# Four kinds of transposes moved from TensorE to VectorE blocks and HBM, in a four-layer graph network

## The chip, the cores and the metric

The kernel runs on one core of one Trainium2 chip. The metric is the device time of one execution in microseconds (us), median of several runs. The engines of the core are named PE (TensorE; PEld is its weight load), DVE (VectorE), ACT (ScalarE), POOL (GpSimd) and SP (SyncE, which here only issues DMAs). All data are float32.

## The reference, cut to what matters

Four layers, each followed by a residual and a normalization over the 128 features; 32 batches of 256 nodes.

```python
x = _layernorm(x + _L0_gnn_ref(x, adj, ...))      # gated neighbours and biases
x = _layernorm(x + _L1_gnn_ref(x, adj, ...))      # two linear maps, two norms over all rows
x = _layernorm(x + _L2_gnn_ref(x, adj, W, a))     # attention
x = _layernorm(x + _L3_gnn_ref(x, adj, ...))      # two graph maps, then LSTMs over windows of 1 to 4
# _L2_gnn_ref
Wh = h @ W;  s1 = Wh @ a1;  s2 = Wh @ a2
e = s1[:, :, None] + s2[:, None, :]
e = where(e >= 0, e, 0.2 * e);  e = where(adj == 0, -inf, e)
out = softmax(e, axis=-1) @ Wh
# _L3_gnn_ref
h = relu(adj @ (x @ Wg0 + bg0));  h = relu(adj @ (h @ Wg1 + bg1))
for p in 1..4:
    last = lstm_p(h cut in windows of p nodes)     # p steps, each needs the one before
    h[every p-th node] = last
```

## The kernel before

The 32 batches are 8 groups of 4 (`GB`). One group is 128 partitions x 1024 elements: 8 tiles of 128x128, two halves of nodes for each of 4 batches. Layers 0 and 1 run first for all groups (they need norms over all rows), to about 144 us. Then the attention of groups 0 and 1 runs alone (the front, to about 188 us). Then come the turns: `slots(slot)` calls `slot(s, ...)` for s = 2 to 10, and in turn s four groups are in work at once: the attention of group s (functions `a_...(s)`), the two graph maps of layer 3 of group s-1 (`a_spread0`, `a_weigh0`, `a_weigh1`, `a_spread1`), the LSTM of group s-2 (11 steps k = 0 to 10; `lstm_x` is the input part and `lstm_h` the state part of the gates, written x(k) and h(k) below) and the last norm of group s-3 (`t_...`). Turns 2 to 7 have an attention, turns 8 and 9 have only what is left; turn 9 splits each LSTM step into two lanes.

An LSTM step goes PE (gates, PSUM `QQ`), ACT (L1200, tanh of the gates), DVE (L1680 to L1690, cell), ACT (L1236, tanh of the cell), DVE (L1708, state), and then PE again. Every engine runs its instructions in the order in which its function `slot` is written, and waits on semaphores. The order of a turn is written out by hand, the same for turns 3 to 7.

In a turn PE also makes four kinds of transposes, each a 128x128 block against the identity `ident`, into PSUM, from where DVE reads them:
- `a_residual` (L680), 8 blocks: the output of layer 1, which lies as features x nodes in `O2T`. DVE adds the residual (L1552, into `Z`), takes statistics (L1400) and dot products with two vectors (L1570); ACT applies the norm (L1042, into `X2`).
- `a_rows` (L729), 8 blocks: the attention's s2, one column per tile, turned into rows of 1024 that stand on all partitions. `a_max` (L1587) reads them.
- `a_turn_e` (L746), 16 blocks: the unnormalized attention weights `E1`. DVE copies them to `MS` (L1608, `a_weights`), and `a_mix` (L767) multiplies with them; `a_project_mix` (L777) follows, `a_sum2_mix` on DVE adds the residual, then come statistics, a power -0.5 on POOL (L446, `rstd`) and the application on POOL (L512, `scale2`), which the next turn's `a_spread0` (L786) reads.
- `t_turn` (L884), 8 blocks: the LSTM's result in `HT`. DVE adds the residual (L1779, `t_sum`), and POOL applies the last norm (L525, `tail`).

SP stores each finished group to the output. Nothing else is moved by DMA in the turns.

## Time and profile before

| what | us |
|---|---|
| median of 3 runs (637.57 to 638.1) | 638.07 |
| the profiled execution | 637.48 |
| its span, first to last instruction | 635.7 |
| PE busy in that span | 621.7 (98%) |
| DVE, ACT, POOL busy | 469.7, 433.1, 168.9 |
| granted TensorE clock | 0.996 of full speed |

The turns start at 188.4 us; turns 2 to 7 take 57.2 to 57.7 us each, turn 8 takes 50.7 and turn 9 with the end about 52. Busy time of PE is modelled and says that it has work, not that it computes at its peak. In the listings of a timeline a row that has xN stands for N instructions, and the distance from its start to the start of the next row is what they cost when PE never waits.

### The profile page before, as it was taken

The numbers are of one execution on the slowest core, as the hardware profiler recorded it, in microseconds if no ns is written. First come the engines' busy times: TensorE is split into PE (matmuls) and PEld (weight loads), VectorE is DVE, ScalarE is ACT, GpSimd is POOL, SyncE is SP. The second block draws the span as 40 slices with busy tenths as digits, with TensorE's granted clock in tenths as the row PEclk, the third lists the DMA queues.
The fourth block names the chain that finished last, engine by engine and source line by source line (L and its number), as shares of the span: only waits on it lengthen the run. The fifth ranks groups of instructions, "written<-read, shape, count | busy, mean of one in ns | idle before, by whom it ended". The sixth has DMA issues, their size and how long they took to land.

```text
span 635.7 us, 9580 instructions
## 1 busy us (share of the span) xinstructions
PE 621.7 (98%) x2768; PEld 441.7 (69%) x2768; DVE 469.7 (74%) x1623; ACT 433.1 (68%) x995; POOL 168.9 (27%) x228
## 2 busy tenths in 40 slices
PE   9999999999999999999999999999999999999994
PEld 6756656447975687579658766865885687577794
DVE  4999999877857657866886687588668766465656
ACT  3667767866947766785677577657847766546774
POOL 1464551005233002303603240341143032103201
PEclk9999999999999999999999999999999999999998
DMA  8334000000000000000000000000000000000000
GB/s 342 129 123 167 1 1 1 1 0 2 2 1 1 0 2 1 1 2 33 2 0 2 33 2 2 34 2 1 1 33 2 2 32 2 1 1 34 2 35 34
DMA packets 4372, 16.84 MB, mean 26 GB/s; under 512 B 480, under 2 KB 480, under 8 KB 4192
## 3 DMA queue, kind: packets, MB, share of 16 engines
q1 hardware_dynamic: 4320, 16.23, 6.6%
q8 instruction: 22, 0.36, 0.2%
q14 instruction: 30, 0.25, 0.1%
HBM read 12.03 MB, written 4.19 MB: 26 GB/s over the span
## 4 chain that ended last, share of the span: by engine, by line
PE 77%; DVE 3%; ACT 2%; issue 1%; POOL 0%; POOLq 0%; ACTq 0%; DVEq 0%
PE QQ L831 27%; PE QQ L843 15%; PE PA L814 4%; PE PA L786 4%; PE PB L805 2%; PE PB L796 2%; PE PB L667 2%; PE PA L667 2%; PE PB L767 2%; PE PA L767 2%; PE QQ L865 1%; PE PB L884 1%; PE PA L746 1%; PE PB L746 1%; PE QQ L875 1%; PE PA L777 1%
## 5 line engine op out<-in xcount | busy, mean ns | idle before, releaser
L1200 ACT ACTIVATE raw<-QQ,BL 128x256 f32<-128x256 f32 (+2 forms) x279 | 150.3, 559 | 78.5 <-PE QQ L843 39.9
L831 PE MATMUL QQ<-HT,WT 128*128 128x256 f32 (+2 forms) x558 | 183.5, 473 | 0.8 <-DVE HT L1708 0.4
L446 POOL TENSOR_TENSOR RSD<-VAR,pw 128x4 f32<-128x4 f32 (+1 forms) x43 | 62.0, 1443 | 379.1 <-DVE VAR L1422 379.1
L831 PEld LDWEIGHTS QQ<-HT,WT 128*128 128x128 f32 x558 | 103.9, 190 | 58.2 <-issue 29.7
L843 PE MATMUL QQ<-HB,WT 128*128 128x256 f32 (+2 forms) x336 | 100.1, 441 | 0.2
L843 PEld LDWEIGHTS QQ<-HB,WT 128*128 128x128 f32 x336 | 61.2, 190 | 28.8 <-issue 13.4
L1236 ACT ACTIVATE raw<-raw 128x256 f32<-128x256 f32 (+4 forms) x79 | 37.0, 469 | 22.8 <-DVE raw L1690 18.8
L1680 DVE SCALAR_TENSOR_TENSOR raw<-raw 128x256 f32<-128x256 f32 (+2 forms) x60 | 31.9, 532 | 22.7 <-ACT raw L1200 21.9
L1708 DVE SCALAR_TENSOR_TENSOR HB<-raw 128x256 f32<-128x256 f32 (+4 forms) x42 | 19.9, 474 | 25.1 <-ACT raw L1236 25.1
L512 POOL TENSOR_SCALAR X<-four,MEAN,RSD 128x128 f32<-128x128 f32 x64 | 32.8, 526 | 1.6
L1042 ACT ACTIVATE X<-Z,OFF,RSD 128x128 f32<-128x128 f32 x80 | 31.8, 482 | 2.0 <-POOL OFF L452 2.0
L622 PE MATMUL PA<-AHT,X 128*128 128x256 f32 x128 | 29.5, 384 | 1.6 <-ACT X L1042 1.5
L1163 ACT ACTIVATE HB<-HB,EB 128x256 f32<-128x256 f32 x64 | 30.9, 502 | 0.2
L622 PEld LDWEIGHTS PA<-AHT,X 128*128 128x128 f32 x128 | 23.7, 190 | 9.6 <-issue 6.4
L786 PE MATMUL PA<-AD,X 128*128 128x256 f32 x128 | 30.3, 379 | 0.0
L636 PE MATMUL QQ<-one_b,later 128*128 128x512 f32 x64 | 29.1, 598 | 0.2 <-ACT one_b L1071 0.2
L814 PE MATMUL PA<-AD,Y 128*128 128x256 f32 x128 | 29.2, 380 | 0.0
L525 POOL TENSOR_SCALAR four<-HB,MEAN,RSD 128x128 f32<-128x128 f32 x56 | 28.8, 530 | 0.7
L786 PEld LDWEIGHTS PA<-AD,X 128*128 128x128 f32 x128 | 23.8, 191 | 6.8 <-issue 4.1
L814 PEld LDWEIGHTS PA<-AD,Y 128*128 128x128 f32 x128 | 24.2, 190 | 4.3
L1083 ACT ACTIVATE HB<-QQ 128x512 f32<-128x512 f32 x32 | 17.9, 587 | 12.7 <-PE QQ L636 12.5
L599 PE MATMUL PB<-four,AD 128*128 128x512 f32 x56 | 26.1, 609 | 0.0
(249 smaller groups left out, 1173.9 us busy)
## 6 DMA issues: line engine op xcount, KB each, us to landing
four<-in_x SPq DMA_DIRECT2D x8, 512.0 KB, 3.9
raw<-in_xt SPq DMA_DIRECT2D x8, 512.0 KB, 6.3
out<-four SPq DMA_DIRECT2D x7, 512.0 KB, 2.6
WT<-in_lstm SPq DMA_DIRECT2D x1, 2048.0 KB, 9.3
later<-in_later SPq DMA_DIRECT2D x1, 725.5 KB, 10.1
AD<-in_adj SPq DMA_DIRECT2D x2, 256.0 KB, 4.6
out<-four SPq DMA_DIRECT2D x2, 256.0 KB, 2.0
early<-in_early SPq DMA_DIRECT2D x1, 275.0 KB, 4.5
```

What stands on the lines that cost most here:

```text
L446: pool.tensor_tensor(RSD[kk][:, ts], VAR[kk][:, ts], pw[:, ts], ALU.pow).then_inc(ln[k]["rstd"], some)
L512: pool.tensor_scalar(tile_of(X1, g, c, b), nth(f.Z2, t), MEAN[f.kk2][:, t:t + 1], RSD[f.kk2][:, t:t + 1], ALU.add, ALU.mult).then_inc(ln[2 ...
L622: mm = pe.matmul(PA[:, b * NODES:(b + 1) * NODES], tile_of(X1, g, m, b), AHT[:, m, :], start=(m == 0), stop=(m == NC - 1))
L786: mm = pe.matmul(PA[:, b * NODES:(b + 1) * NODES], tile_of(X1, g, m, b), ADJT[:, m, :], start=(m == 0), stop=(m == NC - 1))
L814: mm = pe.matmul(PA[:, b * NODES:(b + 1) * NODES], turned(Y, m, b), ADJT[:, m, :], start=(m == 0), stop=(m == NC - 1))
L831: mm = pe.matmul(steps_view(Q[q], k), WT[:, 0, (p - 1) * 4 + q, :], ht_view(par, k), start=True, stop=(s == 0))
L843: pe.matmul(Q[q][:, 0:nw * GB], WT[:, 1, (p - 1) * 4 + q, :], HS[:, (k - 1) % 2, 0:nw * GB], start=False, stop=True).then_inc(g_ps, 1)
L1042: act.activation(nth(to, t), nth(z, t), ACT.Identity, bias=OFF[kk][:, t:t + 1], scale=RSD[kk][:, t:t + 1]).then_inc(ln[k]["out"], 1)
L1163: e = act.activation(f.E1[:, t], f.E1[:, t], ACT.Exp, bias=f.EB[:, t:t + 1], scale=1.0, accum_out=DEN[:, t:t + 1] if g > 1 else None)
L1200: act.activation(TG[q][:, at:n], Q[q][:, at:n], ACT.Tanh, scale=0.5 if q == G else 0.25, bias=BL[:, p - 1, q:q + 1]).then_inc(g_ok, 1)
L1236: act.activation(TC[:, at:n], CELL[:, at:n], ACT.Tanh, scale=0.5).then_inc(tc_ok, 1)
L1680: dve.scalar_tensor_tensor(out=target[:, 0:n], in0=TG[I][:, 0:n], scalar=1.0, in1=TG[G][:, 0:n], op0=ALU.add, op1=ALU.mult).then_inc(cell_ ...
```

## The change

Four kinds of 128x128 transposes leave PE in turns 2 to 7 (the first three) and 3 to 9 (the LSTM's). Each becomes: a DVE instruction that transposes all 32x32 blocks of a buffer (`STREAM_TRANSPOSE`), a DMA that stores the buffer to a scratch in HBM, a wait of SP for it, and four DMAs of 32 partitions each that load it back with the blocks in their new places. The s2 row goes so too, but small (8 rows of 32 elements out, then one row of 1024 broadcast to 128 partitions into `ROWS`).

```diff
+            def y_through(g):
+                sp.wait_ge(y_blk, g - 1)
+                sp.dma_start(turn_y[g], YD).then_inc(y_put, 16)
+                sp.wait_ge(y_put, 16 * (g - 1))
+                reach(sp, z1_ok, NC * (g - 2))
+                for q in range(P // QUAD):
+                    sp.dma_start(quad_rows(YF, q), quad_source(turn_y[g], q)).then_inc(y_got, 16)
...
+            def r_through(g):
+                sp.wait_ge(r_blk, g - 1)
+                for q in range(P // QUAD):
+                    sp.dma_start(turn_r[g].rearrange("(t q i) -> q t i", t=TILES, i=QUAD)[q],
+                                 S2T[q * QUAD:q * QUAD + TILES, :]).then_inc(r_put, 16)
+                sp.wait_ge(r_put, 64 * (g - 1))
...
+                sp.dma_start(ROWS, turn_r[g:g + 1, :].broadcast_to([P, COLS])).then_inc(r_got, 16)
+            def slot(s, par, A, B, L, T):
+                g = s - 3
+                if T and g < LAST:
+                    t_through(g)
+                if s + 2 < GROUPS:
+                    y_through(s + 2)
+                if A:
+                    e_through(s, 0)
+                    e_through(s, 1)
+                    r_through(s + 1) if s + 1 < GROUPS else None
...
-            def a_residual(g, h=None):
-            def a_rows(g):
-            def t_turn(g, par):
...
                 for b in some:
-                    pe.wait_ge(pt_ok, GB * (g - 1) + b + 1)
+                    pe.wait_ge(e_got, 64 * (2 * (g - 2) + b // 2 + 1))
...
+            def a_s12(g):
...
+                dve.transpose(S2T[:], S12[:, TILES:]).then_inc(r_blk, 1)
...
+            def e_blocks(g, some):
+            def t_blocks(g):
+            def y_blocks(g):
```

The two sums that DVE made from PSUM (L1552, L1779) go to POOL (`y_sum`, `t_sum`, two instructions of 128x512 each), and so does the application of the first norm, eight instructions of ACT (L1042) in a turn (`scale1`). The first norm and the dot products of group s+1 are made in turn s, those of group 2 in the front. The LSTM's factor 0.5 is folded into `a_spread` and the small norm steps. All engines get a new order in a turn; `a_mix` of batch 3 and the projections of batches 2 and 3 move to the turn behind.

Below, the order of PE over the border of two full turns, first before (from the mixes of batches 0 to 2 to the first spread of the next turn). L831 is x(k), L843 is h(k).

```order
L767 MATMUL PB<-HB,X 128x256 x2
L767 MATMUL PA<-HB,X 128x256 x2
L767 MATMUL PB<-HB,X 128x256 x2
L777 MATMUL PB<-later,one_a 128x128 x2
L777 MATMUL PA<-later,one_a 128x128 x2
L843 MATMUL QQ<-HB,WT 128x256 x4
L831 MATMUL QQ<-HT,WT 128x256 x4
L767 MATMUL PA<-HB,X 128x256 x2
L777 MATMUL PB<-later,one_a 128x128 x2
L843 MATMUL QQ<-HB,WT 128x256 x4
L777 MATMUL PA<-later,one_a 128x128 x2
L831 MATMUL QQ<-HT,WT 128x512 x3
```

The same stretch and on to the second spread of the next turn in the changed kernel; there L951 is x(k), L963 is h(k), L889 the mix, L899 its projection, L907 the spread and L917 `a_weigh0`.

```order
L963 MATMUL QQ<-HB,WT 128x256 x4
L951 MATMUL QQ<-HT,WT 128x512 x3
L889 MATMUL PA<-HB,X 128x256 x2
L951 MATMUL QQ<-HT,WT 128x512 x3
L899 MATMUL PB<-later,one_a 128x128 x2
L907 MATMUL PA<-AD,X 128x256 x4
L899 MATMUL PA<-later,one_a 128x128 x2
L951 MATMUL QQ<-HT,WT 128x512 x7
L963 MATMUL QQ<-HB,WT 128x512 x4
L917 MATMUL PB<-one_b,later 128x512
L907 MATMUL PA<-AD,X 128x256 x4
L951 MATMUL QQ<-HT,WT 128x340 x7
```

The transposes at L680, L884 and L729 that stood in this stretch are gone, the last mix and two projections stand in it now, and the second spread stands behind h(3). Next, DVE over the same border in the changed kernel: the small scores (L1984) with their block transpose (L1988), the cell of step 10, the small norm steps of `scale2`'s first half, the state of step 10, the cell of step 0 and the first `a_max` of the new turn (ISA, L2000).

```order
L1984 TENSOR_TENSOR S<-DOT,RSD 128x16
L1988 STREAM_TRANSPOSE S2T<-S 128x32
L2099 SCALAR_TENSOR_TENSOR raw<-raw 128x256
L2105 SCALAR_TENSOR_TENSOR raw<-raw 128x256
L2109 SCALAR_TENSOR_TENSOR raw<-raw 128x256
L1823 TENSOR_TENSOR SUM<-STL 128x8
L1824 TENSOR_TENSOR DIF<-STL 128x4
L1826 TENSOR_TENSOR SQD<-DIF 128x4
L1827 TENSOR_SCALAR MEAN<-SUM 128x4
L1829 SCALAR_TENSOR_TENSOR SQD<-SQD,SUM 128x4
L1833 TENSOR_SCALAR VAR<-SQD 128x4
L2127 SCALAR_TENSOR_TENSOR HT<-raw 128x64x4
L2099 SCALAR_TENSOR_TENSOR raw<-raw 128x512
L2000 ISA HB,MX<-WH,NEG 128x256
```

Before, the small scores and `a_max` stood in one turn, with `a_rows` of PE between them. Last, POOL from the first norm's power for group s+1 to that sum in the next turn. Before:

```order
L446 TENSOR_TENSOR RSD<-VAR,pw 128x8
L525 TENSOR_SCALAR four<-HB,MEAN,RSD 128x128 x8
L446 TENSOR_TENSOR RSD<-VAR,pw 128x4
L512 TENSOR_SCALAR X<-four,MEAN,RSD 128x128 x4
L446 TENSOR_TENSOR RSD<-VAR,pw 128x4
L512 TENSOR_SCALAR X<-four,MEAN,RSD 128x128 x4
```

In the changed kernel (L534 the power, L600 `scale2`, L613 the last norm, L592 the scaling of layer 1's output, L632 `scale1`, L640 `t_sum`, L621 `y_sum`):

```order
L534 TENSOR_TENSOR RSD<-VAR,pw 128x4
L600 TENSOR_SCALAR X<-four,MEAN,RSD 128x128 x4
L534 TENSOR_TENSOR RSD<-VAR,pw 128x8
L613 TENSOR_SCALAR four<-HB,MEAN,RSD 128x128 x8
L592 TENSOR_SCALAR HB<-HB,BN 128x1024
L632 TENSOR_SCALAR X<-Z,MEAN,RSD 128x128 x8
L534 TENSOR_TENSOR RSD<-VAR,pw 128x4
L600 TENSOR_SCALAR X<-four,MEAN,RSD 128x128 x4
L640 TENSOR_TENSOR HB<-HB,X 128x512 x2
L621 TENSOR_TENSOR HB<-HB,X 128x4x128 x2
```

Between the two halves of `scale2` there now stand the last norm, the scaling and the first norm's application.

## Rows read from the trace of the kernel before

**Rows 1.** The page's part 1: busy time of each engine in the span.
```profile
PE 621.7 (98%) x2768; PEld 441.7 (69%) x2768; DVE 469.7 (74%) x1623; ACT 433.1 (68%) x995; POOL 168.9 (27%) x228
```

**Rows 2.** Busy us by stage: stretch, length, PE, PEld, DVE, ACT, POOL, clock, DMA share, GB/s.
```profile
150.00:188.40 38.40, 37.77 (x266) 32.78 (x264) 28.19 (x133) 29.45 (x66) 12.86 (x20) 1.00 0.00 1
...
302.80:360.00 57.20, 57.20 (x250) 41.32 (x250) 43.33 (x154) 39.97 (x91) 15.68 (x23) 1.00 0.03 10
532.70:583.40 50.70, 50.17 (x196) 34.03 (x196) 28.13 (x90) 29.01 (x68) 11.39 (x18) 1.00 0.03 11
```

**Rows 3.** PE's timeline of turn 4: start us, us, line, operation, count.
```profile
303.06 2.74 PE L831 MATMUL QQ<-HT,WT 128*128 128x512 f32 x6
305.64 1.04 PE L680 MATMUL PA<-ident,HB 128*128 128x128 f32 x8
306.51 2.74 PE L831 MATMUL QQ<-HT,WT 128*128 128x512 f32 x6
309.09 1.12 PE L884 MATMUL PB<-ident,HT 128*128 128x128 f32 x8
310.04 1.89 PE L786 MATMUL PA<-AD,X 128*128 128x256 f32 x8
311.77 2.74 PE L831 MATMUL QQ<-HT,WT 128*128 128x512 f32 x6
...
316.07 3.60 PE L831 MATMUL QQ<-HT,WT 128*128 128x512 f32 x8
319.50 3.60 PE L843 MATMUL QQ<-HB,WT 128*128 128x512 f32 x8
322.94 1.04 PE L729 MATMUL PA<-ident,S 128*128 128x128 f32 x8
...
344.87 0.60 PE L746 MATMUL PB<-ident,HB 128*128 128x128 f32 x4
...
346.61 1.89 PE L843 MATMUL QQ<-HB,WT 128*128 128x256 f32 x8
```

**Rows 4.** DVE's groups by line: count, busy us, mean ns, idle before.
```profile
L1608 DVE COPY HB<-PB 128x512 f32<-128x512 f32 x14 | 9.6, 686 | 0.1
...
L1570 DVE CUSTOM_DVE_ANT_0 one_c<-Z,WAR 128x128 f32<-128x128 f32 x48 | 10.6, 282 | 0.0
...
L1552 DVE TENSOR_TENSOR Z<-PA,X 128x1024 f32<-128x1024 f32 x6 | 7.3, 1221 | 0.4 <-PE PA L680 0.4
```

**Rows 5.** DVE's timeline at the start of turn 4.
```profile
304.64 0.43 DVE L1690 SCALAR_TENSOR_TENSOR raw<-raw 128x256 f32<-128x256 f32 x1
...
306.74 0.68 DVE L1680 SCALAR_TENSOR_TENSOR raw<-raw 128x512 f32<-128x512 f32 x1
```

**Rows 6.** POOL's timeline in turns 4 and 5.
```profile
346.03 4.03 POOL L525 TENSOR_SCALAR four<-HB,MEAN,RSD 128x128 f32<-128x128 f32 x8
359.23 1.01 POOL L446 TENSOR_TENSOR RSD<-VAR,pw 128x4 f32<-128x4 f32 x1 [9.16 <-DVE VAR L1422]
360.34 2.48 POOL L512 TENSOR_SCALAR X<-four,MEAN,RSD 128x128 f32<-128x128 f32 x4
...
372.01 2.01 POOL L446 TENSOR_TENSOR RSD<-VAR,pw 128x8 f32<-128x8 f32 x1 [0.44 <-DVE VAR L1422]
```

**Rows 7.** POOL, three lines: count, ns least/median/most, first and last start.
```profile
L478 POOL TENSOR_TENSOR one_a<-one_a,HT x6: 1267/1272/1280, 40.7 to 90.6; 128x512 f32<-128x512 f32 x6
...
L504 POOL TENSOR_SCALAR HB<-HB,BN x7: 1198/1202/1495, 145.4 to 374.4; 128x1024 f32<-128x1024 f32 x7
...
L512 POOL TENSOR_SCALAR X<-four,MEAN,RSD x64: 444/452/1008, 171.2 to 542.9; 128x128 f32<-128x128 f32 x64
```

**Rows 8.** DMA issues of the page's part 6: KB each, us to landing.
```profile
raw<-in_xt SPq DMA_DIRECT2D x8, 512.0 KB, 6.3
out<-four SPq DMA_DIRECT2D x7, 512.0 KB, 2.6
```

More of the change, by code:

```diff
@@ L127, in build @@
         DIAG = late[:, 2, 0:NC * P].rearrange("p (c n) -> p c n", c=NC)
+        YD, YF = late[:, 2, 0:COLS], late[:, 2, COLS:2 * COLS]
+        TD, TF, JUNK, ODD = (O2T[:, k * COLS:(k + 1) * COLS] for k in range(4))
         four = sb("four", [NX, TILES * P])
@@ L552, in _ @@
             scale2(1)
+            scaled(4)
             slots(slot)
@@ L671, in _ @@
                 output1(i, h)
-            def a_residual(g, h=None):
-                pe.wait_ge(half_ok, 1) if (g, h) == (0, 1) else pe.wait_ge(yt_ok, g + 1)
-                reach(pe, z2_ok, TILES * before(g))
-                for b in batches(h):
-                    for c in range(NC):
-                        at = g * COLS + b * NODES + c * P
-                        mm = pe.transpose(turned(front(g).PA, c, b), O2T[:, at:at + P], ident[:])
-                mm.then_inc(y_ps, size(h))
             def a_preload(g, h):
+                pe.wait_ge(out2_ok, 2 * (GROUPS - 1)) if g == 0 else None
                 bs = slice(2 * h, 2 * h + 2)
@@ L1238, in slot, with gate @@
             def slot(s, par, A, B, L, T):
-                def gates(k):
-                    lstm_gates(s - 2, k) if L else None
+                def gate(k, *some):
+                    lstm_gates(s - 2, k, some)
                 def state(k):
-                    lstm_state(s - 2, k) if L else None
-                def cell(k):
-                    gates(k)
-                    state(k)
-                cell(0)
-                cell(1)
-                if s == LAST + 2:
-                    for k in range(LANED, NSTEP):
-                        first, last = STEPS[k][1] == 0 and k > LANED, k + 1 < NSTEP and STEPS[k + 1][1] == 0
-                        lane_gates(k, 0, (O,) if first else None)
-                        lane_state(k, 0)
-                        lane_gates(k, 1)
-                        lane_gates(k + 1, 0, (I, G)) if last else None
-                        lane_state(k, 1)
-                    return
@@ L1863, in slot @@
-                a_stats2(s, 1) if A else None
+                a_max(s, (1,))
+                a_sum2_mix(s - 1, (3,))
+                a_bias(s, 0)
+                t_blocks(s - 3)
+                inner(2)
+                a_max(s, (2,))
+                state(2)
+                a_stats2(s - 1, 1)
+                a_small2(s - 1, 1)
+                y_blocks(s + 2) if Y else None
+                inner(3)
+                state(3)
+                a_biased0(s - 1, 0)
+                t_stats(s - 3)
@@ new lines, in slot @@
+                inner(4)
+                state(4)
+                a_max(s, (3,))
+                e_blocks(s, (0,))
+                a_biased0(s - 1, 1)
+                a_dots(s + 1, 1, 0) if N else None
+                a_bias(s, 1)
+                inner(5)
+                e_blocks(s, (1,))
+                state(5)
+                a_biased1(s - 1, 0)
+                e_blocks(s, (2,))
+                a_biased1(s - 1, 1)
+                inner(6)
+                a_stats1(s + 1, 0) if N else None
```

1018 lines of the change are left out of this document (774 added, 244 removed).

## The prediction, written before the changed kernel ran

> **What bounds the kernel now.** I read the page's first part first: PE is busy for 621.7 of 635.7 us and the next engine, DVE, for 469.7 [rows 1]. A sum over the whole span could hide stages with another limit, so I read busy time by stage. In a full turn PE is busy for all of its 57.20 us, while DVE has 43.33, ACT 39.97 and POOL 15.68 [rows 2]. The reader is to see that no other engine is within 13 us of PE there. In the front (150 to 188.4 us) PE shows 37.77 of 38.40, but part of that is filler matmuls that keep it going while it waits for the softmax chain; that stage is bound by a chain through all engines. Then the timeline of PE in one turn: rows follow each other without a wait, so the distance between starts is the price of a piece [rows 3]. Whatever leaves PE in a turn shortens the turn by that distance, until something else comes late.
>
> **What leaves PE.** By the distances in [rows 3]: the residual's 8 transposes cost 306.51 - 305.64 = 0.87 us; the LSTM's 8 cost 310.04 - 309.09 = 0.95; the attention weights' 16 cost 346.61 - 344.87 = 1.74; the row's 8 (at 322.94) have the shape of the first, 0.87. A full turn loses 4.43 us. Turns 3 to 7 give 5 x 4.43 = 22.2, turn 2 has no LSTM transpose and gives 3.5, turns 8 and 9 give 0.95 each. Sum: **27.5 us**. The moved mixes change turn, not amount. A full turn has then 57.2 - 4.4 = 52.8 us of PE work.
>
> **What DVE gets.** It loses the two sums, 1.22 each, and four copies of 0.69: 5.2 us a turn [rows 4]. It gets two block transposes of 128x1024, four of 128x512 and a tiny one. No row shows a block transpose. The nearest rows are one pass over the same elements, 1.22 for 1024 and 0.69 for 512 [rows 4], which gives 5.2 again; below that lies hardly anything, since a pass touches each element once; above, twice the price (10.4) if a 4-byte element needs two passes. I take one pass, since these rows have the same number of elements and one input like it. DVE stays at 43.3 in a turn of 52.8; with two passes it would be 48.5, still less than PE, but with many more late steps.
>
> **What POOL gets.** Four sums of 1.27 [rows 7] and eight applications (4.03 as in the last norm's eight) [rows 6], 9.1 us: 24.8 of 52.8. The time is there; the order is what matters. PE's second spread of group s-1 needs `scale2`'s second half. Counted from the start of a turn, PE reaches it after x(0) 2.58, a mix 0.86, x(1) 2.58, a projection 0.44, half a spread 1.73, a projection 0.44, x(2) 2.58, x(3) 3.43, h(3) 3.43 and half a weighing 0.86, which is 18.9 us [rows 3] (half a spread is the row at 310.04; a mix has half of its instructions; a projection is four passes over 128 columns, half of the eight transposes; half a weighing is one of three gates of x(0)). POOL starts its chain when DVE has the variance of the first half, which stands behind the cell of step 10. That cell ends at 305.07 in the trace, 2.0 us into the turn [rows 5], the six small steps add 0.9, so 2.9. Then power 1.0, four applications 2.0 to 2.5, power 2.0, eight applications 4.0, scaling 1.2, eight applications 4.0, power 1.0, and two of the next four 1.0: 19.1 to 19.6 us [rows 6, 7]. That is 0.2 to 0.7 behind PE's question, and the other two tiles are another 1.0 later while PE has 0.86 of work: a wait of about 0.5 to 1.
>
> That chain is not cheap to guess, because POOL and DVE disturb each other: one application takes 452 ns in the median and 1008 at most, and four took 2.48 where eight took 4.03 [rows 6, 7]. The Trainium skill says so too ("GPSIMD Engine Reference", Specifications): GpSimd shares its SBUF interfaces with VectorE and meets contention from DVE instructions with two SBUF inputs; the 1008 ns agree with it. If each of the 20 applications before the spread ran like the four at 360.34 (0.62 and not 0.50), the chain would be 2.4 us later.
>
> **What the DMAs ask.** Every way through HBM is two transfers behind each other. A 512 KB store landed in 2.6 us, and a load in a crowd in 6.3 [rows 8]; so 5.2 to 12.6 us for a way. I take 5.2 plus 1 for the wait between and the four issues, since the turns move little now (10 GB/s [rows 2]); with about 4.5 MB more in a turn the queue would be at some 90 GB/s. The weights: batches 0 and 1 are transposed on DVE when the cell of step 5 is done, about 29 us into the turn, and asked for by PE at 39; 10 us of room. Batches 2 and 3: about 39 and 48; 9 us. The residual and the LSTM's result have most of a turn. The tightest is the **row**: DVE has it ready about 1.5 us before the turn ends (behind the state of step 9) and asks for it in `a_max` behind the cell of step 0, which ended at 307.42, 4.4 us into the turn [rows 5]. Room: 5.9 us, against 5.2 to 6.2. I charge a wait of 0.3 that half the turns pass on. Behind `a_max` on DVE stand the states of steps 0 and 1, and for them PE waits at x(2).
>
> **Is the LSTM's chain fast enough?** Turn 8 is the bound: nearly the whole LSTM with little else took 50.7 us and PE was busy for 50.17 of it [rows 2]. So the chain can go at 50.7 or less, and 52.8 is possible, but most of the filler between steps is gone. For exact placement I add 0.3 a turn.
>
> **The front.** DVE gets two block transposes (2.4), 8 statistics and 16 dot products of at most 0.28 each (6.7) and the small steps (1.5), some 10.6 us, where it had 38.4 - 28.2 = 10.2 idle [rows 2, 4]. Turn 2 loses the same work, but DVE is not what bounds turn 2. Ends: nothing if all falls into the gaps, 6 us if over half pushes the chain. I take 1.5, nearest to the low end, since the last dots and the scores stand behind all that PE waits for in the front.
>
> **The sum.** Gains 27.5. Waits: turns 3 to 7 with 1.0 each (spread or contention 0.5 to 0.7, row and steps the rest) 5.0; turn 2 0.5; turns 8 and 9, where a transpose filled a wait, 1.0; front 1.5. Together 8.0. Span 635.7 - 27.5 + 8.0 = 616.2; the profiled execution is 1.8 longer than its span, so 618.0 against its 637.5, and the median is 0.6 above that: **618.6 us**.
>
> **Rivals.**
> 1. *All cover holds.* No new wait anywhere: 618.6 - 8.0 = 610.6. For it: no PE wait in a full turn before. Against it: the 19 us coincidence on POOL.
> 2. *DVE and POOL become the bound through their order.* Contention moves `scale2` by up to 2.4 us, or block transposes need two passes and push the states by about as much: 3 us a turn instead of 1.0, and the front at 4: 618.6 + 10 + 2.5 = 631. The price of a pass is the weakest number here. The Trainium skill ("Vector Engine (DVE) Microarchitecture Reference", the reshape front-end) says that a transpose sustains one element per cycle and lane; no trace of before shows it.
> 3. *The row is late, and the kernel is slower than before.* The mechanism is `a_max` blocking DVE's queue behind the cell of step 0 until the broadcast row is back. If both transfers take the 6.3 us of the crowded loads, the row comes 12.6 - 5.9 = 6.7 us late in each of turns 3 to 7; the five lose 33 instead of 1 or so: 618.6 + 32 = 651. It decides at a way of about 5.9 + 4.2 = 10 us: then five turns lose 21 and, with the other waits, all 27.5 are gone. For it: several small DMAs stand in one queue of SP in order, and out-stores and loads of other buffers stand beside them. Against it: 2.6 us for 512 KB, and this row is 4 KB out.
> 4. *The rule that a 128x128 transpose belongs on TensorE.* As a mechanism here: the transposes on PE cost 0.11 us each and are the cheap part, and every 32x32 route adds a chain that PE ends up waiting for, so that the turn stays at 57: no change, 638. The row against it is that PE alone had no idle time in a turn. The Trainium skill ("VectorE: DVE Perf Modes", Rules for kernel authors) has this rule, to use TensorE if PSUM is an acceptable destination; it compares single instructions, not a full and a half-idle engine.
>
> **How the numbers follow.** Chances: the forecast (613 to 624) 0.50; rival 1 (609 to 613) 0.15; rival 2 (624 to 635) 0.24; no change 0.02; slower by rival 3 0.09. A measurement of this kernel can tell about 0.2%, 1.3 us, from no change. The range takes in rivals 1 and most of 2: 609 to 632. Faster 0.89, same 0.02, slower 0.09.
>
> **What would show it.** No L680, L729, L884, and L746 only in the front; full turns of 53 to 54.5 us; PE waits before the second spread (for POOL's `scale2`) and before x(2); block transposes of 1.1 to 1.3 us for 1024 elements; DVE's idle time before the first `a_max` of a turn ended by a DMA, and under 1 us; ways of 5 to 7 us. Wrong if: a block transpose takes 2 us or more; the idle before `a_max` is over 4 us; full turns are at 56 or more; or the front grows by over 4 us.

## The result and the profile after

| kernel | median, us | ratio to the kernel before |
|---|---|---|
| before (4 runs, 637.57 to 638.1) | 637.83 | |
| changed (4 runs, 628.15 to 629.25) | 628.75 | 0.9857 (0.984 to 0.9874) |

The change brings 9.1 us, where 19.2 were forecast. The time lies in the forecast's range, but less than half of the gain arrived. The page's first part after the change, span and busy time (to be set against [rows 1]):

```profile
span 626.4 us, 9346 instructions
PE 598.7 (96%) x2520; PEld 415.0 (66%) x2520; DVE 484.6 (77%) x1656; ACT 410.4 (66%) x960; POOL 239.9 (38%) x296
```

PE lost 23.0 us of busy time, but the span only 9.3: waits came in. Busy time by stage, the answer to [rows 2]: the front and the turns 3 and 6. Columns: stretch, its length, then busy time of each engine, granted clock, DMA share and GB/s.

```profile
150.00:193.34 43.34, 38.42 (x262) 32.39 (x260) 33.73 (x175) 29.30 (x65) 15.67 (x22) 1.00 0.15 50
246.66:301.62 54.96, 53.55 (x211) 37.26 (x210) 45.16 (x160) 36.45 (x85) 23.75 (x25) 1.00 0.26 87
413.13:468.25 55.12, 53.57 (x212) 37.18 (x211) 43.97 (x159) 36.51 (x85) 25.30 (x32) 1.00 0.23 77
```

The turns now start at 193.34, 246.66, 301.62, 357.86, 413.13, 468.25, 523.60 and 573.81. Against the turns of before, with what left or entered PE in each (the last mix and two projections, 1.74 us, go from turn 2 into turn 3, and so on; group 7's last mix still stands at the end of turn 7, at 522.74, so turn 8 gets the two projections alone). "By waits" is what is left of the difference, not a sum of wait rows:

| stage | length before | after | moved by work | by waits | forecast of waits |
|---|---|---|---|---|---|
| front | 188.45 | 193.34 | 0 | +4.9 | +1.5 |
| turn 2 | 57.19 | 53.32 | -3.5 - 1.74 | +1.4 | +0.5 |
| turns 3 to 7 | 287.11 | 276.94 | -22.2 + 0.86 | +11.2 | +5.0 |
| turn 8 | 50.70 | 50.21 | -0.95 + 0.88 | -0.4 | +0.5 |
| turn 9 | 52.25 | 52.59 | -0.95 | +1.3 | +0.5 |

Work -27.5 and waits +18.3 give -9.2 of the measured -9.3. So the gain was lost in two places, the front and the full turns. PE's waits over the whole changed kernel (engine, line waited for, total, times, longest):

```profile
PE PA L907 <- POOL X L600: 5.0, 7, 1.4
PE QQ L963 <- DVE HB L2127: 2.8, 6, 0.7
...
PE QQ L951 <- DVE HT L2127: 1.5, 1, 1.5
```

The first two stand in the full turns, all but one of their times (the last of the second is in turn 8); the third is in turn 2, at 201.98. Turn 6 on PE, from h(3) (L963 at 427.77) to h(5) (L963 at 440.90):

```profile
427.77 3.60 PE L963 MATMUL QQ<-HB,WT 128*128 128x512 f32 x8
431.21 1.02 PE L917 MATMUL PB<-one_b,later 128*128 128x512 f32 x2
433.02 2.40 PE L907 MATMUL PA<-AD,X 128*128 128x256 f32 x8 [0.79 <-POOL X L600]
435.26 4.17 PE L951 MATMUL QQ<-HT,WT 128*128 128x340 f32 x14
...
440.90 2.56 PE L963 MATMUL QQ<-HB,WT 128*128 128x340 f32 x8 [0.62 <-DVE HB L2127]
```

The second spread (L907) could start at 432.07 and starts at 433.02, and takes 2.24 to the next row where [rows 3] has 1.73, since its tiles arrive one by one: 1.46 us lost. The state part h(5) at 440.90 is 0.78 late. The sum is 2.24. A turn of before took 57.42 (303.06 to 360.49; 57.20 was the length of the window in [rows 2]), so 53.0 us of work are left, and the turn's excess of 2.1 is explained by these two places. POOL in the same turn:

```profile
421.67 4.50 POOL L613 TENSOR_SCALAR four<-HB,MEAN,RSD 128x128 f32<-128x128 f32 x8
426.15 4.06 POOL L632 TENSOR_SCALAR X<-Z,MEAN,RSD 128x128 f32<-128x128 f32 x8
430.18 1.00 POOL L534 TENSOR_TENSOR RSD<-VAR,pw 128x4 f32<-128x4 f32 x1
431.29 2.95 POOL L600 TENSOR_SCALAR X<-four,MEAN,RSD 128x128 f32<-128x128 f32 x4
434.42 2.49 POOL L640 TENSOR_TENSOR HB<-HB,X 128x512 f32<-128x512 f32 x2 [0.18 <-DMA HB<-turn_t]
436.85 2.49 POOL L621 TENSOR_TENSOR HB<-HB,X 128x512 f32<-128x512 f32 x2
```

And DVE, from the norm step that the power at 430.18 needs, to the state of step 4 that h(5) needs:

```profile
429.14 0.24 DVE L1833 TENSOR_SCALAR VAR<-SQD 128x4 f32<-128x4 f32 x1
...
436.94 1.64 DVE L1811 BATCH_NORM_STATS2 STL<-HB 128x6 f32<-128x128 f32 x8 [2.71 <-POOL HB L640]
438.50 1.22 DVE L2099 SCALAR_TENSOR_TENSOR raw<-raw 128x340 f32<-128x340 f32 x1
440.34 0.51 DVE L2127 SCALAR_TENSOR_TENSOR HB<-raw 128x340 f32<-128x340 f32 x1 [0.62 <-ACT raw L1402]
```

The last norm's statistics (L1811) hold DVE's queue for 2.71 us until POOL's sum is done, with the cell of step 4 behind them. And there is a row that I had no explanation for at first: that cell's first instruction (L2099) takes 1.22 us, where the same form takes 0.51 elsewhere.

What the forecast had as unknown prices: the three large kinds of block transposes (busy us, mean ns).

```profile
L2027 DVE STREAM_TRANSPOSE HB<-HB 128x512 f32<-128x512 f32 x24 | 16.9, 704 | 0.0
L2198 DVE STREAM_TRANSPOSE HB<-HT 128x1024 f32<-128x1024 f32 x7 | 14.2, 2025 | 0.0
L2204 DVE STREAM_TRANSPOSE HB<-HB 128x1024 f32<-128x1024 f32 x6 | 7.4, 1236 | 2.1 <-DMA turn_y<-HB 2.1
```

The 512 KB stores to the scratch landed in 2.6 us (attention weights) and 3.5 us (LSTM's result) in the median. The row of s2, rival 3's place: its block transpose ended at 411.92 and `a_max` ran at 417.92, after 0.96 us of idle time; the longest such wait was 1.0 us and the five together 3.3.

### The profile page after: what moved, and what is told of

It reads as the page before. It is cut to its first block and busy times, and to the rows that moved or that the text cites. A ratio compares the mean times of both kernels' runs of the same rounds, so it can differ in the third digit from the quotient of the medians.

```text
span 626.4 us, 9346 instructions
## 1 busy us (share of the span) xinstructions
PE 598.7 (96%) x2520; PEld 415.0 (66%) x2520; DVE 484.6 (77%) x1656; ACT 410.4 (66%) x960; POOL 239.9 (38%) x296
## 5 line engine op out<-in xcount | busy, mean ns | idle before, releaser
L951 PE MATMUL QQ<-HT,WT 128*128 128x256 f32 (+2 forms) x558 | 183.6, 473 | 1.8 <-DVE HT L2127 1.5
L534 POOL TENSOR_TENSOR RSD<-VAR,pw 128x4 f32<-128x4 f32 (+1 forms) x43 | 58.5, 1360 | 277.2 <-DVE VAR L1833 185.7
L951 PEld LDWEIGHTS QQ<-HT,WT 128*128 128x128 f32 x558 | 104.6, 190 | 59.5 <-issue 33.5
L963 PE MATMUL QQ<-HB,WT 128*128 128x256 f32 (+2 forms) x336 | 100.0, 441 | 2.8 <-DVE HB L2127 2.8
L963 PEld LDWEIGHTS QQ<-HB,WT 128*128 128x128 f32 x336 | 62.5, 190 | 33.9 <-issue 11.7
L2099 DVE SCALAR_TENSOR_TENSOR raw<-raw 128x256 f32<-128x256 f32 (+2 forms) x60 | 36.1, 601 | 30.3 <-ACT raw L1366 30.0
L1402 ACT ACTIVATE raw<-raw 128x256 f32<-128x256 f32 (+4 forms) x79 | 37.2, 470 | 18.2 <-DVE raw L2109 10.1
L600 POOL TENSOR_SCALAR X<-four,MEAN,RSD 128x128 f32<-128x128 f32 x64 | 45.0, 715 | 1.5
L907 PE MATMUL PA<-AD,X 128*128 128x256 f32 x128 | 32.1, 388 | 5.4 <-POOL X L600 5.0
L907 PEld LDWEIGHTS PA<-AD,X 128*128 128x128 f32 x128 | 22.9, 190 | 15.1 <-POOL X L600 11.3
L613 POOL TENSOR_SCALAR four<-HB,MEAN,RSD 128x128 f32<-128x128 f32 x56 | 31.4, 573 | 0.7
L1811 DVE BATCH_NORM_STATS2 STL<-HB 128x6 f32<-128x128 f32 x88 | 18.4, 278 | 12.5 <-POOL HB L640 12.5
```

Source lines behind the costliest of these rows:

```text
L534: pool.tensor_tensor(RSD[kk][:, ts], VAR[kk][:, ts], pw[:, ts], ALU.pow).then_inc(ln[k]["rstd"], some)
L600: pool.tensor_scalar(tile_of(X1, g, c, b), nth(f.Z2, t), MEAN[f.kk2][:, t:t + 1], RSD[f.kk2][:, t:t + 1], ALU.add, ALU.mult).then_inc(ln[2 ...
L613: pool.tensor_scalar(OUT[:, par, t * P:(t + 1) * P], ZF[:, t * P:(t + 1) * P], MEAN[2][:, t:t + 1], RSD[2][:, t:t + 1], ALU.add, ALU.mult) ...
L907: mm = pe.matmul(PA[:, b * NODES:(b + 1) * NODES], tile_of(X1, g, m, b), ADJT[:, m, :], start=(m == 0), stop=(m == NC - 1))
L951: mm = pe.matmul(steps_view(Q[q], k), WT[:, 0, (p - 1) * 4 + q, :], ht_view(par, k), start=True, stop=(s == 0))
L963: pe.matmul(Q[q][:, 0:nw * GB], WT[:, 1, (p - 1) * 4 + q, :], HS[:, (k - 1) % 2, 0:nw * GB], start=False, stop=True).then_inc(g_ps, 1)
```

## The experiments

All are built on the changed kernel, unless said otherwise. My first theory for the missing gain had three causes: (1) in the front, DVE's in-order queue stands twice at data on its way through HBM and POOL; (2) the second spread waits because `scale1` stands ahead of `scale2`'s second half on POOL; (3) h(5) waits because `t_stats` holds DVE's queue. Rivals: the added work itself, contention of POOL and DVE, and the LSTM's chain.

### 1. The order in the front

The rows of the front on DVE in the changed kernel, both waits 6.0 us together:

```profile
157.07 1.25 DVE L2204 STREAM_TRANSPOSE HB<-HB 128x1024 f32<-128x1024 f32 x1 [2.05 <-DMA turn_y<-HB]
163.92 0.87 DVE L1811 BATCH_NORM_STATS2 STL<-Z 128x6 f32<-128x128 f32 x4 [3.98 <-POOL Z L621]
```

```diff
             a_max(0, (0,))
-            y_blocks(3)
...
-            a_stats1(2, 0)
             a_max(0, (3,))
             a_weights(0, (0,))
+            y_blocks(3)
...
             a_max(1, (1,))
+            a_stats1(2, 0)
             a_sum2(0, (1,))
+            a_stats1(2, 1)
```

> The changed kernel with VectorE's order in the front alone altered: the block transpose y_blocks(3) stands behind the first attention weights of group 0 (before: ahead of them, where it waited 2.05 us for the first transfer's store), and the statistics a_stats1(2, ...) stand behind a_max of group 1 (before: ahead of a_weights(0), where they waited 3.98 us for GpSimd's sum of the data that comes back through HBM). Nothing is left out. My theory: the front lost 4.9 us to these two waits, because everything behind them in VectorE's in-order queue feeds the softmax chain; the kernel becomes 3 to 5 us faster than the changed kernel, 624 to 626 us, with the first turn starting at 189 to 190.5 us. Rival, the front lost its time to VectorE's and GpSimd's added work itself (some 10.6 us of it, in any order): under 1 us gained, 628 or more. Second rival, the statistics come too late now and the first turn waits for them instead: the same 628 or slower.

Measured: 626.88 us, 0.9827 (0.9813 to 0.9842) of before, 1.9 us under the changed kernel, where 3 to 5 were expected. Both waits are gone from the trace, but in their place DVE waits 2.84 us for PE's transposes of the weights (PB L867). The traces agree if the front is counted from its first `a_max`, since what lies ahead of it varies: from there to the first turn it takes 33.7 us before (154.74 to 188.45), 39.1 in the changed kernel (154.24 to 193.34) and 37.4 here (155.10 to 192.51). The order cost some 2 us; the other 3 to 4 of the front had another cause.

### 2. The statistics behind the cell

```diff
                 a_biased0(s - 1, 0)
-                t_stats(s - 3)
                 inner(4)
...
                 a_biased1(s - 1, 1)
+                t_stats(s - 3)
                 inner(6)
```

> The changed kernel with one move in turns 3 to 7: the last norm's statistics t_stats(s-3), which wait on VectorE for GpSimd's t_sum, stand behind a_biased1(s-1, 1) and not ahead of the cell of step 4. Nothing is left out. My theory: in turn 6 of the changed kernel the state part of step 5 came 0.78 us late because VectorE stood 2.71 us at those statistics ahead of that cell; without it 0.6 to 0.9 us a turn come back, 3 to 4.5 us in all: 624 to 626. Rival, the LSTM's chain itself is what the turns of 55 us run at (too little filler between its steps), and the wait only moves to the next step: within 1 us of 628.75.

Measured: 625.59 us, 0.9809 (0.9793 to 0.9826), 3.2 us under the changed kernel. PE's wait for the state (DVE HB) fell from 2.8 us in 6 to 0.2 in 1, and turn 6 from 55.12 to 54.29. The state of step 4 is no longer late; cause 3 holds.

### 3. `scale2` first

```diff
-                scale1(s)
                 rstd(2, 1, s - 1, 1)
                 scale2(s - 1, 1)
+                scale1(s)
                 t_sum(s - 3)
```

> The changed kernel with one move in turns 3 to 7: on GpSimd the eight applications of the first norm (scale1(s), 4.06 us in turn 6) stand behind the second half of scale2(s-1) and not ahead of it. Nothing is left out. My theory: the second spread waits for the last applications of scale2 because GpSimd's queue is too long ahead of them; with 4 us less ahead the small norm steps of VectorE (done at 429.4 in turn 6, where the applications began at 431.29) bound it, 1 to 1.5 us a turn come back, 5 to 7 us in all: 622 to 624. Rival, contention between VectorE and GpSimd makes the applications slow wherever they stand and the wait before the spread stays: 1 us or less gained, 628. Second rival, the first norm's output, now some 2.9 us later, is missed by its own readers, TensorE's scores of group s: slower than 628.75.

Measured: 650.75 us, 1.0206 (1.0191 to 1.0221): 22 us slower than the changed kernel. PE's waits:

```profile
PE QQ L963 <- DVE HB L2127: 20.3, 6, 4.2
PE PA L907 <- POOL X L600: 1.0, 3, 0.4
```

The wait for the spread went from 5.0 to 1.0, as expected. But `scale1` had covered the time until DVE has the variance; now POOL is idle there for 2.8 us and does `scale1` afterwards. `t_sum` starts 23.8 us into the turn (391.54, turn 5 starts at 367.74) instead of 21.3 in turn 6 of the changed kernel, and DVE's queue stands for it:

```profile
394.06 1.65 DVE L1811 BATCH_NORM_STATS2 STL<-HB 128x6 f32<-128x128 f32 x8 [5.07 <-POOL HB L640]
395.62 1.20 DVE L2099 SCALAR_TENSOR_TENSOR raw<-raw 128x340 f32<-128x340 f32 x1
```

So cause 2 was half right: the order made the wait, but the move shifted the price to the state part, where it is larger.

The waits alone do not make the 22 us. PE's waits for the state grew by 17.5 us and those for the spread shrank by 4.0. The rest is the TensorE clock: behind each wait of 3.6 to 4.2 us the granted clock falls, and h(5) runs at the lower of the two levels for all or most of its time. In turn 5 it takes 3.93 us from its start to the next row, and in turn 6 it takes 4.69, where it takes 2.40 in the changed kernel (440.90). The row of turn 5, and the windows of both rows (behind POOL's column stands the granted clock):

```profile
398.01 4.10 PE L963 MATMUL QQ<-HB,WT 128*128 128x340 f32 x8 [4.24 <-DVE HB L2127]
```

```profile
398.01:401.94 3.93, 3.93 (x8) 2.50 (x9) 3.48 (x17) 2.56 (x7) 0.00 (x0) 0.60 0.39 118
457.17:461.86 4.69, 4.69 (x8) 2.85 (x9) 3.80 (x18) 3.08 (x8) 0.00 (x0) 0.50 0.00 0
```

0.50 of full speed is the level of 1.2 GHz. Over turns 3 to 7, h(5) and the rows behind it are 10 us longer than at full clock. So nearly half of the loss is not waiting but slow work after it.

### 4. All three

> The three moves of the runs beside this one together: VectorE's order in the front, the last norm's statistics later, scale2's second half ahead of the first norm's applications. Nothing is left out. My theory: the three waits are at different places and add up: 10 to 13 us, 616 to 619. If the LSTM's chain, without filler, holds the full turns at about 54 to 55 us, the two moves in the turns give little together and this lands at 622 to 625, about what the front alone gives; then the gain off TensorE was bounded by that chain.

Measured: 641.84 us (nine executions, 638.67 to 642.49), 1.0052 (1.0036 to 1.0068). Neither branch of the expectation. `t_stats` no longer stands ahead of the cell here, yet PE waits 3.47 us for the state of step 4. DVE and POOL around it:

```profile
390.14 4.49 DVE L2127 SCALAR_TENSOR_TENSOR HB<-raw 128x340 f32<-128x340 f32 x1 [1.50 <-ACT raw L1402]
```

```profile
389.35 2.49 POOL L640 TENSOR_TENSOR HB<-HB,X 128x512 f32<-128x512 f32 x2
391.80 2.46 POOL L621 TENSOR_TENSOR Z<-HB,X 128x512 f32<-128x512 f32 x2
```

A DVE instruction of 0.51 us took 4.49, from just after POOL began its first sum until POOL ended its fourth (394.26). This is the row at 438.50 again, larger. New theory: a POOL sum of two SBUF inputs keeps out a DVE instruction with two SBUF inputs. The clock falls here too: h(5) behind the wait takes 3.99 us at a granted clock of 0.59 in turn 5 (394.69), and four of the five full turns have such a stretch, 7.9 us longer in all than at full clock. Against the 623.51 us of experiment 6, 14.5 us of longer waits for the state, 3.6 of shorter waits for the spread and these 7.9 make 18.8 of the 18.9 us between the two spans.

### 5. The exclusion by itself

Ten stages behind the end of the changed kernel, each begun when DVE and POOL are both through with the one before; one execution.

```diff
+            ON_POOL = [None, lambda: pairs(4), lambda: singles(8), lambda: pairs(6), lambda: pairs(6), lambda: pairs(6),
+                       lambda: singles(8), lambda: singles(8), lambda: pairs(6), None]
...
+            ON_DVE = [lambda: twos(6), None, None, lambda: twos(10), lambda: stats(24), lambda: turns(10), lambda: twos(6),
+                      lambda: stats(14), lambda: banked(10), strided]
```

> The changed kernel with ten short stages behind its end, each begun when both VectorE and GpSimd are through with the one before: 1 VectorE alone, 6 instructions with two SBUF inputs (scalar_tensor_tensor, 128x512); 2 GpSimd alone, 4 sums of 128x512; 3 GpSimd alone, 8 applications (tensor_scalar) of 128x128; 4 both, 10 of the first and 6 sums; 5 VectorE 24 statistics of 128x128 (one input) beside 6 sums; 6 VectorE 10 block transposes of 128x512 beside 6 sums; 7 VectorE 6 of two inputs beside 8 applications; 8 VectorE 14 statistics beside 8 applications; 9 VectorE 10 with one input in SBUF and one in PSUM beside 6 sums; 10 block transposes of 128x1024 alone, two contiguous, two with a source stride of 16 bytes, two with a destination stride of 16 bytes. Theory: in stage 4 the two exclude each other, and VectorE's share is done only while GpSimd is not at a sum, so the stage takes the sum of both (7 + 7.5 us) or VectorE waits up to 7 us; in stages 5, 6, 8 and 9 both run as alone (one SBUF input); in stage 7 GpSimd waits: its 0.45 us become 1.0 and more. Rival, it is bandwidth: then both slow by a similar share in stages 4 to 8, whatever the number of inputs. Stage 10: 1.23 and 2.03 us for the first two forms as in the trace; by a price per element touched the third is like the second.

DVE, stages 1, 4, 5, 6, 7, 9 and 10:

```profile
625.57 3.71 DVE L2528 SCALAR_TENSOR_TENSOR HB<-HB 128x512 f32<-128x512 f32 x6 [2.27 <-DMA out<-four]
...
638.02 12.50 DVE L2528 SCALAR_TENSOR_TENSOR HB<-HB 128x512 f32<-128x512 f32 x10 [3.47 <-POOL X L716]
650.56 4.74 DVE L2534 BATCH_NORM_STATS2 HB<-HB 128x6 f32<-128x128 f32 x24
658.08 6.05 DVE L2540 STREAM_TRANSPOSE HB<-HB 128x512 f32<-128x512 f32 x10 [2.78 <-POOL X L710]
665.61 3.79 DVE L2528 SCALAR_TENSOR_TENSOR HB<-HB 128x512 f32<-128x512 f32 x6 [1.48 <-POOL X L710]
...
675.89 6.07 DVE L2546 SCALAR_TENSOR_TENSOR HB<-HB,PA 128x512 f32<-128x512 f32 x10 [0.84 <-POOL X L716]
683.44 2.37 DVE L2556 STREAM_TRANSPOSE HB<-HB 128x1024 f32<-128x1024 f32 x2 [1.48 <-POOL X L710]
685.73 3.80 DVE L2558 STREAM_TRANSPOSE HB<-HB 128x1024 f32<-128x1024 f32 x2
689.46 3.73 DVE L2560 STREAM_TRANSPOSE HB<-HB 128x1024 f32<-128x1024 f32 x2
```

POOL, stages 2, 3, 4, 5 with 6, 7 (two rows), 8 and 9:

```profile
629.35 4.92 POOL L710 TENSOR_TENSOR X<-X 128x512 f32<-128x512 f32 x4 [3.03 <-DVE HB L2528]
634.45 3.47 POOL L716 TENSOR_SCALAR X<-X,MEAN,RSD 128x128 f32<-128x128 f32 x8 [0.18 <-POOL X L710]
638.07 10.11 POOL L710 TENSOR_TENSOR X<-X 128x512 f32<-128x512 f32 x6
650.61 14.90 POOL L710 TENSOR_TENSOR X<-X 128x512 f32<-128x512 f32 x12 [2.43 <-DVE HB L2528]
665.68 3.88 POOL L716 TENSOR_SCALAR X<-X,MEAN,RSD 128x128 f32<-128x128 f32 x2 [0.18 <-POOL X L710]
669.54 2.60 POOL L716 TENSOR_SCALAR X<-X,MEAN,RSD 128x128 f32<-128x128 f32 x6
672.32 3.47 POOL L716 TENSOR_SCALAR X<-X,MEAN,RSD 128x128 f32<-128x128 f32 x8 [0.17 <-POOL X L716]
675.93 7.40 POOL L710 TENSOR_TENSOR X<-X 128x512 f32<-128x512 f32 x6
```

Alone, a DVE instruction with two SBUF inputs takes 0.62 us, a POOL sum 1.23 and a POOL application 0.43. Ten of the first beside six sums (stage 4): 12.5 us for DVE's 6.2, and 10.1 for POOL's 7.4; the stage takes nearly the 13.6 of both one after the other. Read singly, the two take turns: POOL's sums start 1.67 us apart (639.80, 641.47, 643.13 and on), and so do DVE's instructions (638.63, 640.31, 641.97 and on). DVE needs 1.7 us for 0.62 of work, more than twice; sharing at half speed each would give 1.24. Beside statistics, block transposes or an instruction with its second input in PSUM, POOL's sums stay at 1.24 and DVE at its own pace.

In stage 7 DVE's six two-input instructions run in 3.79 us, nearly as alone (3.71), and POOL gets only two applications done meanwhile, in 3.88; the other six, when DVE is through, take 0.43 each. So a POOL application can wait for several DVE instructions in a row, as it can the other way round in experiment 4, and the expectation (1.0 and more each) held with 1.9. It is exclusion, and it came only where the DVE instruction has two SBUF inputs; the rival (bandwidth, every pair slowed) falls. The Trainium skill ("SBUF — State Buffer", Who interferes with whom) has this rule: the port pair that DVE and GpSimd share is taken for a whole instruction, and the other blocks. Stages 4 and 7 agree with it.

What the stages do not explain is how long the other is kept out: in stage 4 DVE gets in after each sum, while in experiment 4 one DVE instruction stood through four sums (4.49 us). What decides between the two was not tested.

### 6. Both moves that gained, and the sums on DVE

> The two moves that gained when made alone, together: VectorE's order in the front (alone 626.88 us) and the last norm's statistics behind the cell of step 5 (alone 625.59); the changed kernel has 628.75. Nothing is left out. Theory: they are waits at different places, so the gains of 1.9 and 3.2 add up: 623.7. Rival, the two are one and the same drift of the LSTM's chain: the better of the two, 625.6.

Measured: 623.51 us, 0.9776 (0.9761 to 0.9791). The gains add up, within 0.2 us.

The next kernel has the three moves of experiment 4, with `t_sum` and `y_sum` of turns 3 to 7 on DVE:

```diff
+            def y_sum(g):
+                dve.wait_ge(y_got, 64 * (g - 1))
...
                 a_biased0(s - 1, 0)
+                y_sum(s + 1) if N else None
                 inner(4)
...
+                t_sum(s - 3)
                 t_stats(s - 3)
                 inner(6)
```

> The kernel with all three moves (641.84 us) with one thing changed: in turns 3 to 7 the sums of the residual and of the LSTM's result (four instructions of 128x512, two inputs in SBUF) are made by VectorE and not by GpSimd. Nothing is left out. What the trace of the three moves shows: the state of step 4 on VectorE took 4.49 us where it takes 0.51, from 390.14 to 394.63, and GpSimd's four sums ran from 389.35 to 394.26. Theory: a GpSimd sum keeps a VectorE instruction with two inputs from running until GpSimd is through with what is queued; that is what cost the three-move kernel 18 us against 623.7. With the sums on VectorE (2.4 us of it a turn, in its idle time) the wait of 3.5 us a turn for the state goes, and the wait for the second spread stays gone: 617 to 622. Rival, the state was late because the first norm's output or the LSTM's result came late: then 638 or more stays. Second rival, VectorE's 2.4 us push its chain: 623 to 627.

Measured: 623.77 us, 0.9781 (0.9764 to 0.9797), 18.1 us under the three moves with the sums on POOL. The 3.5 us waits are gone and with them the low clock (0.999 over the span, 0.985 with the sums on POOL), and PE waits 1.0 us for the spread in all. A wait of 0.87 us a turn for the state of step 6 came in, since sum and statistics now stand ahead of its cell; the one theory's 617 to 622 became the second rival's 623.8.

### 7. How much was PE's work worth?

The kernel before, with most transposes of the four kinds left out from turn 2 on:

```diff
                 for b in batches(h):
                     for c in range(NC):
+                        if g >= 2 and (b, c) != (GB - 1, NC - 1):
+                            continue
                         at = g * COLS + b * NODES + c * P
                         mm = pe.transpose(turned(front(g).PA, c, b), O2T[:, at:at + P], ident[:])
```

> The kernel before with most of the four kinds of transposes left out from turn 2 on, and nothing put in their place: 7 of 8 at L680, L729 and L884 and 3 of 4 at L746 are missing; the copies and sums that read them stay and read what lies in PSUM. By the distances of rows 3, 3.66 us leave PE in a full turn, 2.8 in turn 2 and 0.8 in turns 8 and 9, together 22.8. Theory, PE is the bound and the LSTM's chain holds at turns of 53.5 us: the time falls by 20 to 23 us, to 615 to 618. Rival, with these transposes gone the LSTM's steps have too little filler between them and PE waits for the states: 620 to 626, and the changed kernel's 628.75 would be near what could be had.

Measured: 631.06 us, 0.9896 (0.9881 to 0.9911) of before (637.70 in this comparison): 6.6 of 22.8 us. The rival holds, and more strongly than it said. A full turn went from 57.42 to 56.67, by 0.75 of 3.66. PE waits at four places of turn 4 (0.51, 0.64, 0.39 and 0.21 us); the middle two are shown, and the last row is x(1) of turn 5, the place of the first:

```profile
308.97 2.84 PE L835 MATMUL QQ<-HT,WT 128*128 128x512 f32 x6 [0.64 <-DVE HT L1712]
322.63 4.27 PE L835 MATMUL QQ<-HT,WT 128*128 128x340 f32 x14 [0.39 <-DVE HT L1712]
...
360.31 2.84 PE L835 MATMUL QQ<-HT,WT 128*128 128x512 f32 x6 [0.51 <-ACT raw L1204]
```

By the turn's length 2.9 of the 3.66 us come back; 2.7 of them stand between the rows of turn 4, as time in which PE waits for the LSTM's gates and states. These transposes were filler between steps: the old order gets a turn only to 56.67 without them, the changed kernel gets it to 54.3 with the way through HBM (experiment 2). That the new order alone makes this difference is not shown: the changed kernel also takes eight applications off ACT in a turn (busy 39.97 before, 36.51 in turn 6), and no run has the old order with a lighter ACT.

### 8. The front with less work for DVE

```diff
-                    dve.bn_stats(STL[kk][:, t, :], nth(z, t)).then_inc(ln[k]["stats"], 1)
+                    dve.bn_stats(STL[kk][:, t, :], nth(z, t)[:, 0:16] if (k, g) == (1, 2) else nth(z, t)).then_inc(ln[k]["stats"], 1)
...
+                        n = 16 if g == 2 else P
```

> The kernel of the first run of this call with less work for VectorE in the front: the statistics and the 16 dot products of group 2 are taken over 16 and not 128 of the features (so group 2's first norm and scores are left out in part); all instructions, waits and ways stay. Theory, the front's remaining 3 us over the kernel before are VectorE's added work (it is busy nearly without a gap from 162 to 180 us): some 3 us of it go, and 1.5 to 2.5 us come off the time. Rival, the front is held by the way through HBM or by GpSimd's sum and application: under 0.5 us.

"The kernel of the first run" is the one of 623.51 us. Measured: 622.07 us (621.87 to 624.53), 0.9762 (0.9743 to 0.9781), 1.4 us less; the first turn starts at 190.63 instead of 192.24. DVE's added work is a cause, at the low end of what I expected. It does not reach the 188.45 of before; what holds the last 2 us was not settled (single executions differ by up to 0.9 us ahead of the front's first `a_max`, at 154.2 to 155.1).

### 9. Statistics later still, and two tests on that kernel

```diff
                 t_sum(s - 3)
-                t_stats(s - 3)
                 inner(6)
...
                 state(7)
+                t_stats(s - 3)
```

> The kernel with the sums on VectorE (623.77 us) with one move in turns 3 to 7: the last norm's statistics (1.65 us on VectorE) stand behind the state of step 7 and not ahead of the cell of step 6. Nothing is left out. In its trace the input part of step 9's neighbour at 448.82 waits 0.87 us for the state of step 6, and sum and statistics ran ahead of that cell from 443.16 to 446.04, while the gates were ready at 444.5. Theory: 0.8 to 0.9 us a turn come back, 4 to 4.5 us: 619.3 to 620. A full turn then has 52.8 us of work and 0.4 us of waits. Rival, the LSTM's chain is at its limit and the wait reappears at a later step: 622.5 or more.

Measured: 620.60 us (619.95 to 621.01), 0.9738 (0.9723 to 0.9752): the fastest kernel here. Turns 5 and 6 take 53.70 us and the wait at 448.82 is gone. A wait of 0.3 at another state came in. Against the 623.51 us of experiment 6 this kernel has three things more, `scale2` first, the sums on DVE and the statistics behind step 7; the first two with the statistics ahead of step 6 gave nothing (623.77), so the 2.9 us came only with all three.

In the next two expectations "the kernel of the first run" is the one of 620.60 us.

> The kernel of the first run of this call with one more move in turns 3 to 7: the block transpose of the LSTM's result (2.03 us on VectorE) stands behind the small norm steps of scale2's second half and not ahead of the cell of step 2. Nothing is left out. Theory: the wait for the second spread (0.35 us in a full turn now) goes, since the small steps are 2 us earlier: 1 to 1.7 us off. Rival, the second spread is not held by the small steps but by nothing that can be seen at 0.35 us, and the block transpose now stands ahead of the cell of step 3, which has 1.5 us of idle time before it: within 0.7 us of the first run.

Measured: 623.57 us, 0.9788 (0.9772 to 0.9804), 3 us slower than 620.60. The rival's place was right and its size too small, for a reason that neither text had. In turns 3 to 5 the block transpose of layer 1's output stands there too, so that 3.2 us of block transposes follow each other ahead of the cell of step 3 (turn 5: 371.80 for 2.05 us and 373.76 for 1.21), where the kernel of 620.60 had 0.36 us of idle time left (at 371.51). PE waits 1.2 to 1.6 us for that state, and the turns are 0.6 to 1.1 us longer. Turns 6 and 7 have no such second transpose; there the moved one (426.60, 2.07 us) costs less than 0.1. The 1.5 us of idle time in the expectation were read in turn 6. The theory stays untested: the small steps end 15.8 us after the turn's start in both kernels, since DVE, without the transpose ahead of them, waits for ACT instead. The spread takes 2.14 us to the next row, 2.07 before the move.

> The kernel of the first run of this call with every projection behind a mix (L899 of the changed kernel, 24 in turns 2 to 8) made twice, the second over the first: TensorE gets 24 times 0.44 us more, 10.6 us, and nothing else changes. Theory, in the new order TensorE is the bound of the full turns: 9 to 10.6 us longer. Rival, the chain of LSTM steps is the bound and TensorE has hidden slack between the rows: under 6 us. (The kernel before gave back only 6.7 of 22.8 us when its transposes were left out.)

Measured: 628.30 us, 0.9861 (0.9847 to 0.9876): 7.7 of 10.6 us. Between both expectations. Turns 5 and 6 grew by 1.33 each, for 1.76 of work; the missing 0.43 are the small waits that the work now fills. Added to the new order, PE's work counts for three quarters; taken out of the old one, it counted for 0.29. The two are not the same test: nothing was added to the old order or taken out of the new one, and a full engine can give little back and still cost the full price of what is added.

## Why the forecast was off, step by step

The step that failed is the term for the waits: the sum had 8.0 us of them, and 18.3 came. Of the 10.3 us between, the full turns make 6.2 (11.2 for 5.0) and the front 3.4 (4.9 for 1.5). Three of the four signs of being wrong appeared: a block transpose of 2 us (the LSTM's, 2.03), a full turn over 56 (turn 4, 56.24) and a front over 4 us longer (4.9). That the time lies in the range is due to the range's taking in most of rival 2.

- **What bounds the kernel: failed as a statement on gains.** "Whatever leaves PE in a turn shortens the turn by that distance, until something else comes late" was true with the second half at once: with 3.66 us gone and the old order, 2.9 came back (experiment 7). No wait of PE in a full turn did not mean that there was slack behind it. The 57.20 us of a full turn were the window's length; the turn has 57.42, and 53.0 without the transposes.
- **What leaves PE: right.** The transposes at L680, L729 and L884 are gone and L746 stays only in the front. The work by the distances, 27.5, was taken over into the balance; no run checks it by itself.
- **What DVE gets: partly.** One pass for contiguous data was right (1.24 and 0.70 for 1.22 and 0.69). The LSTM's block transpose takes 2.03 instead of 1.22, since it reads with a stride; that is 0.8 us a turn. It stands ahead of the small norm steps, but moving it behind them (the second kernel of experiment 9) did not bring them earlier.
- **What POOL gets: the place was right, the size not.** The second spread waited, as worked out, but lost 1.46 us in turn 6 and not 0.5 to 1. The applications just ahead of it took 0.74 each. What I called contention has a form: exclusion of two-input instructions. It also hits DVE, which the forecast did not charge at all: eight DVE rows in the turns are longer than the median of their form by 5.9 us together. Four of them are the 0.7 us ahead of h(5) in turns 3 to 6, and one (0.86 us, at 198.68) stands ahead of the state that PE waits for in turn 2.
- **The mis-sized term** is the wait of the full turns, 1.0 each where 2.2 were measured. Its missing part is h(5): I named who waits for DVE's states at x(2), but not that `t_stats` waits for POOL's new sum with a cell behind it. The rule that I had written for `a_max` holds for every wait on DVE's queue.
- **What the DMAs ask: right in what it cost.** The way of the row took 6.0 us (5.2 to 6.2 forecast), its waits were 1.0 at most, and rival 3 did not occur. The way of the LSTM's result took 9.4 us, longer than the sum had, and was hidden.
- **Is the LSTM's chain fast enough? Right for the new order only.** Turn 8 showed that the chain can go at 50.7, and 53.70 was reached; but that says nothing of a given order.
- **The front: failed.** 4.9 instead of 1.5: 1.9 by the order, 1.4 by DVE's work, the rest open.
- **Rivals.** Rival 2 was the one that came (631 for 628.75), by order and exclusion, not by two passes; that its number is so near is partly luck, since it had 3 us of waits in a full turn and 4 in the front, and 2.2 and 4.9 came. Rival 4 was refuted in its mechanism: at x(2), where a late row would show, PE waits in no full turn. Its result, a turn that stays near 57, is what the old order gives when the transposes merely go.

## To carry to other kernels

When a full engine is relieved, leave the work out once without any replacement: what comes back as waits is the price of the chain in that order. On in-order queues, ask for each new wait what stands behind it, and put consumers of another engine's new result behind the steps that a loop depends on. Before work is moved from VectorE or ScalarE to GpSimd, count which instructions beside it have two SBUF inputs. When a kernel gets slower by more than its waits, look at the granted clock behind the longest one.
